# A four-layer graph network: the third layer's bias moved to TensorE as a product with a row of ones, and VectorE's two sums over products joined into one

## What is computed

```python
def _edgeconv(x, edge_index, edge_attr, ln_g, ln_b, We, be, Wr, bias):
    h = relu(_layernorm(x, ln_g, ln_b))
    src, dst = edge_index
    w = (edge_attr @ We + be).reshape(-1, 16, 8)
    msg = einsum('ei,eio->eo', h[src], w)
    agg = segment_sum(msg, dst, num_segments=N)
    return agg + h @ Wr + bias            # (N, 8)
# both directions of each edge, each with its own weights, 8 numbers each
out = concatenate([_edgeconv(..., edge_index, ...n), _edgeconv(..., edge_index[:, ::-1], ...r)], -1)
```

## Time and profile before

| | |
|---|---|
| median of 3 runs | 4018.26 us (4015.35 to 4021.06) |
| the profiled execution | 4015.06 us, its span 4013.3 us |
| mean granted TensorE clock | 0.734 of full speed |
| third layer's edge loop | about 2343 to 2946 us of the span |

### The profile page before, as it was taken

The page is one execution under the profiler, slowest core; times in us unless marked ns, Lnnn a source line. Parts: engine busy times, 40 slices in busy tenths (PEclk is TensorE's granted clock), DMA queues, the critical chain, the costliest instruction groups (busy, mean ns, idle before and its releaser), DMA issues.

```text
span 4013.3 us, 28541 instructions
## 1 busy us (share of the span) xinstructions
PE 1919.0 (48%) x7574; PEld 1368.4 (34%) x7574; DVE 2771.8 (69%) x4103; ACT 1182.7 (29%) x2921; POOL 2718.9 (68%) x2767
## 2 busy tenths in 40 slices
PE   1200025555410000566665047777723666669998
PEld 0000013443300000445553036666513555554444
DVE  9991026666672000678786978988987888878898
ACT  1010013333340000445553344444523444430111
POOL 4777777777777777777774057766705777756777
PEclk6555557777755555788887578888866888889999
DMA  6011013333541000233335223333442333341110
GB/s 189 9 45 36 8 43 121 121 121 120 106 135 36 5 5 5 76 116 118 116 117 117 87 83 109 113 108 111 110 156 77 119 120 119 122 103 43 32 37 28
DMA packets 192773, 345.55 MB, mean 86 GB/s; under 512 B 81018, under 2 KB 159466, under 8 KB 164067
## 3 DMA queue, kind: packets, MB, share of 16 engines
q1 hardware_dynamic: 103104, 287.51, 19.5%
q0 software_dynamic: 81344, 21.38, 7.8%
q10 hardware_dynamic: 8164, 34.85, 2.3%
HBM read 66.26 MB, written 277.24 MB: 86 GB/s over the span
## 4 chain that ended last, share of the span: by engine, by line
POOL 53%; issue 18%; PE 14%; DVE 13%; DMA 1%; SPq 1%; ACT 0%; POOLq 0%; DVEq 0%
POOL rows L507 31%; POOL edges_by_dst L489 9%; POOL edges_by_src L489 9%; PE psK L586 6%; DVE natS L1239 6%; PE psX L734 5%; PE psX L645 2%; POOL natD L531 1%; DVE h L1129 1%; DVE natS L1369 1%; DVE psX L1126 1%; POOL x L527 1%; POOL x L519 1%; PE psK L715 1%; DMA rows<-table,rec 0%
## 5 line engine op out<-in xcount | busy, mean ns | idle before, releaser
L507 POOL DMA_INDIRECT rows<-table,rec x1760 | 1670.9, 949 | 865.3 <-issue 526.3
L586 PE MATMUL psK<-work 128*128 128x256 f32 x2640 | 816.9, 475 | 637.3 <-DVE work L1219 309.8
L586 PEld LDWEIGHTS psK<-work 128*128 128x128 f32 x2640 | 634.3, 248 | 800.5 <-issue 667.1
L860 ACT ACTIVATE work<-iota,rec 128x128 f32<-128x128 f32 x1760 | 536.2, 391 | 588.5 <-PE psK L586 342.8
L1239 DVE SCALAR_TENSOR_TENSOR natS<-natS,keep,psK 128x256 f32<-128x256 f32 x1069 | 513.5, 480 | 70.6 <-PE psK L586 29.8
L1219 DVE TENSOR_TENSOR work<-at_hi,psX 128x2048 f32<-128x2048 f32 x220 | 502.3, 2283 | 4.2 <-ACT psX L905 0.4
L489 POOL DMA_INDIRECT edges_by_dst<-natD,pos x391 | 375.4, 960 | 168.5 <-issue 126.9
L489 POOL DMA_INDIRECT edges_by_src<-natS,pos x391 | 375.2, 960 | 127.1 <-issue 127.1
L734 PE MATMUL psX<-natD,work 128*128 128x512 f32 x784 | 348.3, 596 | 17.6 <-DMA work<-scan_by_column 9.5
L531 POOL TENSOR_TENSOR natD<-natS 128x512 f32<-128x512 f32 x196 | 244.3, 1265 | 118.6 <-DVE natS L1369 118.6
L654 PE MATMUL psX<-ident,natD 128*128 128x128 f32 x220 | 38.7, 303 | 587.5 <-DVE natD L1251 587.2
(11 more groups left out here) (157 smaller groups left out, 2605.2 us busy)
## 6 DMA issues: line engine op xcount, KB each, us to landing
scan<-natS SPq DMA_DIRECT2D x110, 1024.0 KB
scan<-natD SPq DMA_DIRECT2D x28, 1024.0 KB
scan_by_column<-work SPq DMA_DIRECT2D x28, 1024.0 KB
rows<-table,rec POOLq DMA_INDIRECT x1760
scan<-work SPq DMA_DIRECT2D x27, 1024.0 KB
scan_by_column<-natS SPq DMA_DIRECT2D x27, 1024.0 KB
table<-h ACTq DMA_DIRECT2D x28, 896.0 KB, 3.6
work<-scan SPq DMA_DIRECT2D x126, 128.0 KB, 2.0
```

Source lines behind the costliest of these rows:

```text
L507: pool.indirect_dma_start(out=rows[k][:, u * D:(u + 1) * D], out_offset=None, in_=table.ap(), in_offset=bass.IndirectOffsetOnAxis(ap=rec[k ...
L586: k = nc.tensor.matmul(psK[:, o:o + BW], lo, spread[par][:, o:o + BW], start=True, stop=True)
L860: a = S.activation(to[:, t * P:(t + 1) * P], iota1[:, :], ACT.Abs, bias=field(l, g % RING, LO[ORDER[l]])[:, t, :])
```

## The change

The bias is no longer spread over 128 partitions in bias16. One partition holds eight copies of the 16 bias numbers (bias8, 16 small loads where there were 2), and another tile holds 128 ones (one_row, one more memset at the start). After the two root products of a block, TensorE makes a third one of 1 row by 128 (one_row) with 1 row by 128 (bias8), accumulated into the same numbers of psR. VectorE's L1313 and the wait ahead of it are gone. VectorE's products of both directions are stored interleaved, so that one reduce of 1152 numbers takes the place of the two of 576.

```diff
-        bias16 = sb("bias16", [P, D])
+        bias8 = sb("bias8", [1, 8 * D])
+        one_row = sb("one_row", [1, P])
...
-        CLEARED = 12
+        CLEARED = 13
...
-        WEIGHTS = 16 * (2 + 8 * 13)
+        WEIGHTS = 16 * 8 * 15
...
-                load(bias16[:, 0:HALF], bias_n_in[None, :].to_broadcast([P, HALF]), weights)
-                load(bias16[:, HALF:D], bias_r_in[None, :].to_broadcast([P, HALF]), weights)
                 for v in range(8):
+                    load(bias8[0:1, v * D:v * D + HALF], bias_n_in[None, :], weights)
+                    load(bias8[0:1, v * D + HALF:(v + 1) * D], bias_r_in[None, :], weights)
...
                     for b in range(root_block(g)[1]):
                         for s in range(2):
-                            kk = nc.tensor.matmul(psR[:, b * P:(b + 1) * P],
-                                                  rootT[:, (2 * s + b) * P:(2 * s + b + 1) * P],
-                                                  Wroot[s], start=s == 0, stop=s == 1)
+                            nc.tensor.matmul(psR[:, b * P:(b + 1) * P],
+                                             rootT[:, (2 * s + b) * P:(2 * s + b + 1) * P],
+                                             Wroot[s], start=s == 0, stop=False)
+                        kk = nc.tensor.matmul(psR[:, b * P:(b + 1) * P], one_row[0:1, :], bias8[0:1, :],
+                                              start=False, stop=True)
                     kk.then_inc(root_s["sums"], 1)
...
+            clear(one_row[:, :], 1.0)
...
-                            V.tensor_tensor(prod[:, m * 288:(m + 1) * 288]
-                                            .rearrange("p (u o t) -> p u o t", o=HALF, t=A9),
+                            V.tensor_tensor(prod[:, 0:G * D * A9]
+                                            .rearrange("p (u s o t) -> p s u o t", s=2, o=HALF, t=A9)
+                                            [:, side, 4 * q:4 * q + 4, :, :],
...
-                        for side in range(2):
-                            own.did(V.tensor_reduce(v3(raw[par])[:, :, side * HALF:(side + 1) * HALF],
-                                                    prod[:, side * 576:(side + 1) * 576]
-                                                    .rearrange("p (u o t) -> p u o t", o=HALF, t=A9), AX.X, ALU.add))
+                        own.did(V.tensor_reduce(raw[par], prod[:, 0:G * D * A9].rearrange("p (n t) -> p n t", t=A9),
+                                                AX.X, ALU.add))
...
                     V.tensor_tensor(xs, xs, psR[:, 0:nb * P], ALU.add).then_inc(root_s["added"], 1)
-                    dve.wait_ge(root_s["added"], g + 1)
-                    V.tensor_tensor(v3(xs), v3(xs), bias16[:, None, :].to_broadcast([P, nb * 8, D]), ALU.add)
```

## The result

The changed kernel takes 4138.98 us (median of 6 runs, 4137.42 to 4142.99); the kernel before took 4016.81 us in the same comparison. The ratio is 1.0303, with a 95% interval from 1.0293 to 1.0314. So it is slower, as forecast, but by 122 us where 34 were forecast, and outside the stated range. The span of its profiled execution is 4136.2 us.

The account below looks back on a forecast made before the run. The prediction took a TensorE-VectorE ring in the third layer's loop as the bound in most turns; +35.2 - 1.5 + 0.2 = +33.9 us on 4018.26 gave 4052 us. Own range 4044 to 4063 (chance 0.62), wider range 4028 to 4064 (0.80).

Parts of the forecast that it names:

- The ring: Third layer's loop: TensorE and VectorE wait for each other (L1311, L645, L586, L1239), 11.09 us a turn with two blocks.
- the price of one bias product: Added product on TensorE between the wait for `added` and L586: 0.40 us each, +35.2 us in all.
- case D: Third layer's loop: full 0.43 us for every bias product and L1296 late; 4063 to 4070 us, chance 0.06.
- A second term: Three early turns bound by VectorE: each saves 0.44 + 0.05 us, added products don't reach the end; -1.5 us.
- main term: Bias products on TensorE in the third layer's loop: 30.4 us in 38 two-block turns, 4.8 in 12 one-block turns.
- a longer turn is a turn with more time at the low rate: Third layer's loop: turns of different length hold the same high time, 6.8 to 6.9 us; added products pay the low-clock price.
- Rival B: Third layer's loop: busier TensorE keeps its clock, VectorE bounds at 9.74 us a turn; 3960, or 3990 if half; chance 0.08.
- The rule on weight loads: TensorE's weight loads take time by columns, not rows, so a one-row product costs as the others and the sum stays.
- L1313's removal and the joined reduce at nothing: VectorE in the third layer's loop: both hidden beside TensorE in TensorE-bound turns, worth nothing there.
- Rival A: Third layer's loop: clock rises where it does now, each bias product costs 0.24 us; 4038 us, chance 0.18.
- rival C: Third layer's loop: a one-row product costs next to nothing, 0 to 8 us for 98; 4017 to 4026, chance 0.06.
- Setup: Start of the kernel: one more memset delays SyncE's first load by at most 0.3 us; +0.2 us.

Follow-up runs that it names:

- e1: The kernel before with only the joined reduce and interleaved store, bias staying on VectorE; 4017.94 us, ratio 1.0.
- e6: The kernel before without any bias: L1313 and its wait left out, no product in its place; 4022.78 us, ratio 1.0001.
- e2: The changed kernel with two reduces as before, so only the bias moved to TensorE; 4139.64 us, ratio 1.0305.
- e7: The kernel before with VectorE's root step moved ahead of its run of sums; 3988.44 us, ratio 0.9923.
- e8: The changed kernel with VectorE's root step moved ahead of its run of sums; 4018.32 us, ratio 0.999.
- e4: The changed kernel with the two one-row products of a turn next to each other; 4108.73 us, ratio 1.023.
- e5: The kernel of e3 with the bias product over 64 rows in place of 128; 4141.42 us, ratio 1.0305.
- e3: The changed kernel with the bias product padded to 128 rows, bias in one partition and zeros in the rest; 4053.75 us, ratio 1.009.
- e9: The kernel of e3 with a second 128-row product for each block, its moving operand all zeros; 4015.61 us, ratio 0.9993.
- e10: The kernel of e3 with VectorE's root step moved ahead of its run of sums; 3974.22 us, ratio 0.9891.

## Where the prediction was right and where it was wrong

**The ring was right.** VectorE's half is worth nothing (e1, e6), TensorE's half is all of it (e2), all but 3 us of it lies in the third layer's loop, and taking the root products off the ring gave the gain that it should (e7: 35 us for 33 worked out).

**The step that failed is the price of one bias product.** The prediction took it from "a root product of the same 128 columns with 128 rows", between 0.37 and 0.43 us, and held 0 to be the other end. That row prices a product that looks like its neighbours. The one that was added costs 0.95 us at 1.2 GHz and 0.58 at 2.4 GHz (e8), because TensorE loses 0.59 us at the low clock in the excursion from the full array to a part of it and back (e4), and as much with 64 rows as with one (e5). The rows show where: in a row of full products a weight load starts 0.21 us ahead of its product, and at a change of shape it starts with it, behind 0.22 us in which the loader does nothing. Below, the unknown product was bounded at 0; above, it had no bound of its own, and case D, dearer than thought, went no further than 0.43 (and its terms, 50 x 0.1 to 50 x 0.2 on top of that, come to 4060 to 4065 and not to 4063 to 4070).

**A second term had the wrong sign.** The three early turns stood at -1.5 us, because VectorE set them and the added products there "don't reach the end". They took 10.0 us more: in the changed kernel they are turns of 13.57 us like the others. That they ran at a clock of 1.00 was taken as given, and it went with the change.

**With the right price the rest of the sum would have stood nearer.** For a product of 128 rows the same sum was right in its main term: e3's turns of 11.95 us lie in the forecast 11.7 to 12.0, and its 38 turns with two blocks took 31.7 us more for 30.4 forecast. That the total came within 2 us of 4052 is partly luck: e3's three early turns took 5.8 us more where -1.5 was forecast, and its last 11 turns 1.3 where 4.8 was. The one-row price puts 0.95 in place of 0.40: 38 x 2 x 0.95 + 12 x 0.95 = 84 us, less than 122. Turn for turn, 13.65 - 11.09 = 2.56 us, of which 2 x 0.95 = 1.90 is the products, 2.04 by e4's price; 0.5 to 0.7 is left.

**What is left is, for the most part, the clock.** The high time of a turn stayed at 6.8 us, as argued, but less of TensorE's work lies in it. In the changed kernel the clock is at 1.00 all through VectorE's run of sums, when TensorE has little to do, and into the start of the root stage, then 0.50 for most of L587; TensorE is busy for 4.19 us of such a high stretch (2714.66 to 2721.49). In four high stretches in a row of the kernel before (2612.30 to 2649.85) it is busy for 4.19, 4.19, 4.78 and 5.09 us, 4.56 on average. The 0.37 us that no longer lie there take twice as long at half the clock, which by this estimate is another 0.37 us a turn. That part of the working, "a longer turn is a turn with more time at the low rate", holds for this kernel and e3, but it isn't a law: e9 has longer work than e3 and more high time.

**Rival B was dismissed too easily.** It said that a busier TensorE keeps its clock. For the kernel as changed it is refuted (0.75, lower than before). With full products its clock came true in e9 (0.93), where I expected turns of 12.8 us and 4085 at best; its time did not, 4015.61 us and a ratio of 0.9993 where B had 3960 to 4010. The reason given against it, that the stretch of VectorE's sums "is not changed", was not enough. In the Trainium skill ("TensorE: Matmul & The Clock Gate", What's actually happening) activity releases the throttle; e9 agrees with it (0.93). How it fits the changed kernel, no row decides: there the records show TensorE busy in 6.70 of 6.70 us at a clock of 0.50, and only then does the clock rise.

**The rule on weight loads was beside the point.** By the Trainium skill (same page, LDWEIGHTS (loading the stationary operand)) a load takes its time by columns. The load of L649 means 263 ns and that of L646 256, so the trace agrees for the length of the load; what changed is when it starts. The 190 and 297 ns that the prediction set side by side don't compare rows, nor waiting for the array: nearly all loads of L606 lie at the high clock and most of L645 at the low one, and at one level they are alike (186 and 190 ns at 2.4 GHz, 333 and 328 at 1.2).

**Smaller points.** 196 more PE records: right (7574 to 7770). L1296 waiting in most turns: right, 46. VectorE idle before L1243 in more turns than 37: right, 55. Turns with one block at about 10.6 us: wrong, the last 11 average 11.5. A clock a little below 0.81: wrong, 0.75. L649 as long as L646: wrong where it matters, its pair of records has 0.79 us at the low clock for 0.63 in e3. L1313's removal and the joined reduce at nothing: right. Rival A (4038) and rival C (4017 to 4026) are refuted by the price. Setup: SyncE's first load starts at 2.92 for 2.66, 0.26 us as reckoned.

**What stays open.** Why the low stretch lasts 6.8 us in every turn was not separated further: whether it is the stalls, the unused rows of the array, or the length of the stage. In e5 half of the rows are used and the turns are as with one row, which speaks against the rows, and isn't proof. Of the 2.56 us a turn 0.15 to 0.3 are in neither of the two terms above. And only products of 128 columns in fp32, with rows counted from the first partition, were tried.

## What to carry to other kernels

Before work is moved off an engine, find out whether that engine is late at this place: here the removed step was free (e6), and the added one lay on the ring that sets the turn. A product over fewer rows than its neighbours isn't a cheap product; in a stream of full ones, as far as this case goes (fp32, 128 columns), pad it to the full array (85 us here), put narrow ones side by side (30 us), or take it off the path (121 us, e8; 165 us padded as well, e10). When an operation's shape isn't in the trace, bound its price from above too, and count the clock it may cost.

## What was not expected of the hardware

- A product of 1 row between products of 128 rows (fp32, 128 columns) costs 0.95 to 1.02 us at 1.2 GHz and 0.58 at 2.4 GHz, one with 128 rows 0.43 at 1.2; with 64 rows the stage is as long as with one (2.91 and 2.90 us). The records of the narrow pair say little of it (0.79 us for 0.63); the loss shows in the distance to the next start, and in the weight loads, which start with their products where they start 0.21 us ahead in a row of full ones.
- TensorE recorded as busy without a gap for 6.70 us can stay at a granted clock of 0.50, and with full products alone for 5.87 us (kernel before).
- Adding 98 full products of zeros took 38 us off the kernel (e3 to e9), with a clock of 0.93 for 0.79. Whether products of other numbers than zeros would do the same was not tried.
